# A two-layer graph network with residual norms on one core: source indices kept on chip, GpSimd's gathers written out over all groups, four input buffers in place of two

## What is computed

```python
def _cgconv(x, src, dst, attr, Wf, bf, Ws, bs):
    z = jnp.concatenate([x[dst], x[src], attr], axis=-1)
    m = jax.nn.sigmoid(z @ Wf + bf) * jax.nn.softplus(z @ Ws + bs)
    return jax.ops.segment_sum(m, dst, num_segments=N) + x

h = leaky_relu(graph_norm(_cgconv(x, ...)))        # layer 1
h = leaky_relu(graph_norm(_cgconv(h, ...)))        # layer 2
x = layernorm(x + h)
Wh = x @ W + b                                     # layer 3
Wr, Wc = Wh[src], Wh[dst]
sim = sum(Wr * Wc) / max(|Wr| * |Wc|, eps)
base = adj_v * softplus(deg_coeff[0] * deg_v + deg_coeff[1]) * (src != dst)
pos = segment_sum(base * relu(sim) * Wc, src); neg = segment_sum(-base * relu(-sim) * Wc, src)
out = layernorm(x + scale * (c[0] * pos + c[1] * neg + c[2] * Wh))
```

## Time and profile before

| | us |
|---|---|
| median of 3 runs | 11558.24 |
| lowest, highest run | 11554.88, 11572.58 |
| span of the profiled execution, first to last instruction | 11550.1 |
| GpSimd (POOL) busy | 7691.0 (67%) |
| TensorE (PE) busy | 4750.4 (41%) |
| VectorE (DVE) busy | 4365.6 (38%) |
| ScalarE (ACT) busy | 2260.1 (20%) |

### The profile page before, as it was taken

The page is one execution under the profiler, slowest core; times in us unless marked ns, Lnnn a source line. Parts: engine busy times, 40 slices in busy tenths (PEclk is TensorE's granted clock), DMA queues, the critical chain, the costliest instruction groups (busy, mean ns, idle before and its releaser), DMA issues. The chain is left out here.

```text
span 11550.1 us, 89590 instructions
## 1 busy us (share of the span) xinstructions
PE 4750.4 (41%) x15982; PEld 2985.0 (26%) x15982; DVE 4365.6 (38%) x7054; ACT 2260.1 (20%) x3460; POOL 7691.0 (67%) x6875
## 2 busy tenths in 40 slices
PE   0067776777206666777641222222222222222221
PEld 0033333333103333333321222222222222222221
DVE  2333333333303333333333344444444444444445
ACT  0033333333103333333321101001001010010100
POOL 5556656555435665666653688888888888888885
PEclk9977778878557777777775555555555555555555
DMA  7233333333203333333320233333333333333333
GB/s 278 66 93 97 96 97 96 96 96 94 89 25 87 93 93 89 93 94 91 93 72 20 32 36 37 36 36 37 36 37 36 36 37 36 37 36 36 37 36 75
DMA packets 869598, 790.23 MB, mean 68 GB/s; under 512 B 483674, under 2 KB 621802, under 8 KB 868298
## 3 DMA queue, kind: packets, MB, share of 16 engines
q0 software_dynamic: 398432, 244.82, 17.4%
q1 hardware_dynamic: 461928, 480.85, 13.7%
q10 hardware_dynamic: 9218, 64.36, 1.4%
HBM read 547.94 MB, written 241.38 MB: 68 GB/s over the span
## 5 line engine op out<-in xcount | busy, mean ns | idle before, releaser
L659 POOL DMA_INDIRECT by_src<-arena,put_idx x1568 | 2483.8, 1584 | 482.0 <-issue 482.0
L583 POOL DMA_INDIRECT G<-h_rows,idx x1568 | 1542.1, 983 | 978.2 <-issue 480.6
L583 POOL DMA_INDIRECT G<-in_x,idx x1470 | 1452.8, 988 | 971.0 <-issue 469.5
L760 PE MATMUL ps_gv<-ident,arena 128*128 128x128 f32 x1568 | 385.4, 427 | 3729.8 <-issue 3709.7
L583 POOL DMA_INDIRECT G<-wh_rows,idx x1568 | 1530.0, 976 | 484.3 <-issue 443.1
L760 PEld LDWEIGHTS ps_gv<-ident,arena 128*128 128x128 f32 x1568 | 307.5, 224 | 3790.6 <-issue 3769.7
L1036 DVE TENSOR_TENSOR_SCAN xd_t<-same,xd_t,ps_inj 128x512 f32<-128x512 bf16 x588 | 751.6, 1278 | 1377.5 <-remote 951.5
L712 PE MATMUL ps_gv<-attr,w_attr 65*128 65x512 f32 x1568 | 1089.0, 832 | 391.0 <-DMA attr<-in_attr_t 361.7
L715 PE MATMUL ps_gv<-arena,w_src 128*128 128x512 f32 x1568 | 1034.6, 797 | 0.0
L1179 DVE TENSOR_SCALAR put_idx<-arena,drop 128x8 int32<-128x8 f32 x196 | 45.5, 232 | 2269.4 <-DMA by_src<-arena,put_idx 2269.4
L1059 DVE TENSOR_SCALAR arena<-ps_gv 128x512 f32<-128x512 f32 x392 | 267.5, 682 | 1624.8 <-remote 1071.3
(11 more groups left out here) (161 smaller groups left out, 7026.5 us busy)
## 6 DMA issues: line engine op xcount, KB each, us to landing
inj<-first_edge_rows SPq DMA_DIRECT2D x588, 256.0 KB
running_sums<-arena SPq DMA_DIRECT2D x392, 256.0 KB
same<-same_dst SPq DMA_DIRECT2D x1176, 64.0 KB
first_edge_rows<-zeros ACTq DMA_DIRECT2D x56, 896.0 KB
attr<-in_attr_t SPq DMA_DIRECT2D x392, 128.0 KB
same_sum<-same_dst SPq DMA_DIRECT2D x784, 64.0 KB
G<-h_rows,idx POOLq DMA_INDIRECT x1568
G<-wh_rows,idx POOLq DMA_INDIRECT x1568
```

Of the source, the lines that this page charges most:

```text
L583: pool.indirect_dma_start(out_, None, table_in, bass.IndirectOffsetOnAxis(ap=index, axis=0)).then_inc(s, 16)
L659: pool.indirect_dma_start(acc_d[a], bass.IndirectOffsetOnAxis(ap=put_idx[:, buf, k:k + 1], axis=0), put[:, buf, k * D:(k + 1) * D], None, ...
L760: mm = pe.transpose(spread[:, buf, k], src_f[:, buf, k:k + 1].to_broadcast([P, P]), ident[:])
```

## The change

- `src_idx`, 128 x 1568 int32, takes all source indices in the first load of the kernel. The 588 loads of `idx` go, and the 14 of `src_ahead`. GpSimd's gathers take columns of `src_idx` that are fixed numbers, so its program is written out: 196 groups without a loop in each of the three passes, and the 14 steps of the gather ahead.
- `inj`, `same`, `attr` and `G` have NB = 4 buffers. The other tiles keep two. Loops over groups run 49 trips of 4.
- `same_sum` and its 784 loads go: both scans read `same`. So the second half of `load_rows` waits for the *sums* of group k-2 (`s_sumt`) where it waited for the scan before (layer 3 still waits for the scan).
- SyncE's order in layers 1 and 2: attributes of k+1, rows and flags of k+2, the ahead row of k, the store of the sums of k-3.
- `same_all` moves into the shared arena, which is cut to 16800 columns.

```diff
+            load(src_idx[:], src_g, s_srcs)
             load(last_i, block_last.to_broadcast([P, SEARCH]), s_search)
...
-            load(src_i, src_e, s_edges)
...
                 def load_rows(h, buf):
-                    g = h * 2 + buf
-                    sp.wait_ge(s_scan, done(layer, h, buf, 2))
+                    g = h * NB + buf
+                    sp.wait_ge(s_injt, done(layer, h, buf, NB))
                     load(inj[:, buf], inj_groups[ds(g, 1)].rearrange("a p c -> p (a c)"), s_load[buf])
-                    load_same(same, s_load, g, buf)
+                    sp.wait_ge(s_scan if layer == 2 else s_sumt, done(layer, h, buf, NB))
+                    for half in range(2):
+                        load(same[half * D:(half + 1) * D, buf],
+                             same_groups[ds(g + half * GROUPS, 1), :].to_broadcast([D, COLS]), s_load[buf])
                 def load_ahead(h, buf):
-                    if buf and layer < AHEAD:
-                        sp.wait_ge(s_gt, done(layer, h, buf, 2))
+                    if buf % 2 and layer < AHEAD:
+                        sp.wait_ge(s_gt, done(layer, h, buf, NB))
...
-                pipeline(sp, (load_idx, -1), (load_rows, -1), (load_ahead, 0), (load_attr, 1), (load_again, 2),
-                         (store_sums, 4))
+                load_attr(0, 0)
+                pipeline(sp, (load_attr, -1), (load_rows, -2), (load_ahead, 0), (store_sums, 3))
...
-                with pool.Fori(0, PAIRS) as i:
-                    for buf in range(2):
-                        gather_group(i, buf)
+                for g in range(GROUPS):
+                    gather_group(g)
...
-                        wait(s_idx[buf], h * 16 + 16 * (layer * PAIRS + 1))
-                        if layer < 2:
-                            wait(s_gt, done(layer, h, buf, 2))
-                        else:
-                            wait(s_used, done(0, h, buf, 2))
+                        wait(s_gt if layer < 2 else s_used, done(layer if layer < 2 else 0, h, buf, NB))
...
-                    dve.wait_ge(s_same_sum[buf], loaded_one(32, layer, h))
-                    v.tensor_tensor_scan(sum_t[:, buf], same_sum[:, buf], msg, sum_t[:, 1 - buf, COLS - 1:COLS],
+                    v.tensor_tensor_scan(sum_t[:, buf % 2], same[:, buf], msg, sum_t[:, 1 - buf % 2, COLS - 1:COLS],
```

More of the change, by code:

```diff
@@ L103, in two, with each @@
             return [sem(f"{name}_{i}") for i in range(2)]
+        def each(name):
+            return [sem(f"{name}_{i}") for i in range(NB)]
         def dram(name, shape, dt=F32):
@@ L158, in gnn @@
         seam_row = sb("seam_row", [P, D])
-        idx = sb("idx", [P, 2, SLOTS], I32)
-        inj = sb("inj", [P, 2, SLOTS * D])
-        same = sb("same", [P, 2, COLS], BF16)
-        same_sum = sb("same_sum", [P, 2, COLS], BF16)
-        attr = sb("attr", [2 * DA + 1, 2, COLS])
-        G = sb("G", [P, 2, SLOTS * D])
+        inj = sb("inj", [P, NB, SLOTS * D])
+        same = sb("same", [P, NB, COLS], BF16)
+        attr = sb("attr", [2 * DA + 1, NB, COLS])
+        G = sb("G", [P, NB, SLOTS * D])
         xd_t = sb("xd_t", [P, 2, COLS])
-        arena = sb("arena", [P, 17600])
+        arena = sb("arena", [P, 16800])
         def carve():
@@ L418, in pipeline @@
                     steps.begin(i - head, per)
-                step(i, 0)
-                step(i, 1)
+                for buf in range(n):
+                    step(i, buf)
             if steps:
@@ L423, in pipeline @@
                 steps.begin()
-            for k in range(2 * tail, 2 * pairs + max(lags)):
-                step(k // 2, k % 2)
+            for k in range(n * tail, n * trips + max(lags)):
+                step(k // n, k % n)
             if steps:
@@ L511, in load_same @@
[L511 to L518 removed]
+                    if buf % 2 and layer < AHEAD:
+                        sp.wait_ge(s_gt, done(layer, h, buf, NB))
+                        load(G[:, buf, (SLOTS - 1) * D:],
+                             ahead_pairs[:, ds(h * (NB // 2) + buf // 2, 1)].rearrange("p a f -> p (a f)"),
+                             s_ahead_in[buf // 2])
@@ L520, in store_sums @@
+                def load_attr(h, buf):
+                    sp.wait_ge(s_gates, done(layer, h, buf, NB))
+                    load(attr[0:2 * DA, buf], attr_t[ds(h * NB + buf, 1)].rearrange("a k c -> k (a c)"), s_attr[buf])
                 def store_sums(h, buf):
-                    g = h * 2 + buf
+                    g = h * NB + buf
                     sp.wait_ge(s_sums, done(layer, h, buf))
-                    load(sums_groups[ds(g, 1)].rearrange("a p c -> p (a c)"), sums[:, buf], s_stored[buf])
@@ L585, in gather_ahead @@
             def gather_ahead(begin, end):
-                with pool.Fori(begin, end) as i:
+                for i in range(begin, end):
                     for buf in range(2):
-                        wait(s_aidx[buf], i * 16 + 16)
                         wait(s_ahead_st[buf], i * 16 + 16)
                         for c in range(CH):
-                            gather(agg[:, buf, c * D:(c + 1) * D], x, get_nodes[:, buf, c:c + 1], s_ahead[buf])
+                            pair = (i * 2 + buf) * CH + c
+                            gather(agg[:, buf, c * D:(c + 1) * D], x, src_of(2 * pair + 1, SLOTS - 1), s_ahead[buf])
+            pool.wait_ge(s_srcs, 16)
             pool.wait_ge(s_end_idx, 1)
@@ L624, in _ @@
                     stages.append((lambda h, buf, c=c: put_column(layer, h, buf, c), 0 if layer else 3))
-                pipeline(pool, *stages, pairs=CP)
+                pipeline(pool, *stages, n=2, trips=CP)
                 table_in = (x, h_d, wh_d)[layer]
@@ L655, in add_run @@
                         half = a // (ACCS // 2)
-                        if a % (ACCS // 2) == 0 and (run or buf or not at_start(h)):
+                        if a % (ACCS // 2) == 0 and (run or g):
                             wait(s_added[half], added(h, buf, run))
@@ L1203, in _ @@
             steps.end()
-            with dve.Fori(1, PAIRS) as i:
-                steps.begin(i - 1, 26)
+            with dve.Fori(1, TRIPS) as i:
+                steps.begin(i - 1, 13 * NB)
                 last_layer(i)
-            steps.end(PAIRS - 1, 26)
+            steps.end(TRIPS - 1, 13 * NB)
             with dve.Fori(0, CP) as i:
```

226 lines of the change are left out of this document (107 added, 119 removed).

## The result

The changed kernel took 11652.5 us (median of three runs, 11635.7 to 11656.5) against 11558.2 before: 1.0081 of it, 95% interval 1.0058 to 1.0103. It is slower by 0.8%, where I had forecast 1.9% faster (11345). The profiled execution has a span of 11654.7 us, 104.6 more than before.

The account below looks back on a forecast made before the run. It took GpSimd to pace the group passes, TensorE not far behind. Setup -25, first waits -18, straight-line code 0, layer 2 -442, layer 1 +271 sum to -214 against 11550: 11336, taken as 11345 us; range 11060 to 11700.

Parts of the forecast that it names:

- Setup: Start of the kernel: indices become the first load, so GpSimd's gathers ahead start earlier; 25 us off.
- Straight-line code: GpSimd's program without loops in the three passes: neither gain nor loss, taken as 0.
- Layer 1: Layer 1's pass: TensorE waits for the ahead row in odd groups; 27.5 us a pair, 271 us more.
- Layer 2: Layer 2's pass: the index wait goes; 10.6 us a group, 2078 us against 2520, 442 off.
- Layer 3 and the stages: Layer 3's pass stays at 25.4 us a group apart from its first wait; norm stages are left alone.
- Rival 1: Layers 1 and 2: ahead row's chain with late releases outweighs layer 2's gain; 30 us a pair, 11785 us, chance 0.20.
- Rival 3: Layers 1 and 2: late releases, not index loads, make the group times, which remain; 11515 us, chance 0.07.
- Rival 2: Layers 1 and 2 both at GpSimd's pace, the ahead row landing in time; about 10510 us, chance 0.04.
- rival 4: All three passes: each loop trip costs a branch of 1.06 us; 312 us more off, 11030 us, chance 0.03.
- The signs: Profile marks for the forecast, and three against it: no L705 wait, layer 2 above 12 us a group, microsecond steps.
- the first waits: First group of each layer's pass: GpSimd's wait for its first indices goes; together 18 us off.

Follow-up runs that it names:

- e4: Kernel before with only the source indices kept on chip and GpSimd's groups written out without a loop: 11290.2 us, 0.9662 of before.
- e11: The change with the ahead row first in SyncE's order, on chip 9: 11150.2 us, 0.9654 of before.
- e1: The change with the ahead row first in SyncE's order, on chip 1: 11235.4 us, 0.961 of before.
- e3: The change with the ahead row first, and layer 2's two products with w_dst left out: layer 2 took 2341 us.
- e7: The change with the ahead row first and the sums turned a group later, on chip 6: 10620.3 us, 1.0037 of before.
- e17: The change with the ahead row first, GpSimd waiting for src_rows_turned only every second group in layers 1 and 2, chip 11: 10616.4 us, 1.0026 of before.
- e2: The change with the ahead row first, and half of the gathers in layer 2: layer 2 took 1320 us.
- e18: The change with the ahead row first, GpSimd in layers 1 and 2 waiting for earlier gathers to land, chip 11: 11168.9 us, 1.0555 of before.
- e15: The change with the ahead row first, layer 2 making only its products with w_attr, on chip 10: layer 2 took 2290 us.
- e16: The change with the ahead row first, 6 of 8 gathers a group in layer 2, on chip 10: layer 2 took 1784 us.
- e12: The change with the ahead row first and the sums turned a group later, on chip 9: 11136.8 us, 0.9645 of before.

## Why the prediction was wrong

- *Setup*, -25: right (-24.3). *Straight-line code*, 0: right for layer 3 (`e4`), and GpSimd's own steps in layer 2 are 2022 us in both kernels.
- *Layer 1*, +271: right in size (+273.5), in place (L693 of odd groups) and in its parts (9.7 us idle, 27.2 us a pair). `e11` shows the mechanism by taking it away on one chip: 486 us of layer 1 come back (and 459 in `e1` against the first result, on chips that may differ).
- *Layer 2*, -442: this is the step that failed. The sentence "GpSimd's own 10.3 us, if TensorE keeps below it" was true: the own steps came out at 10.3, and TensorE kept below it. Wrong was "I take 10.6 us a group": of the 489 us that GpSimd waited for `idx` or "remote", I let 442 go with the index loads and gave late releases 0.3 us a group. They cost 1.5, 294.8 us of GpSimd's stops in the pass. I had taken the name of a wait for its cause. A stop with the name `idx` was for the greater part a late release, with the index load's own time behind it: with the loads gone there are about as many stops (88 for 94), of 3.4 us in place of 5.3, and `e4`, which takes away the index loads and the loop alone, has 101 of 3.6. So 417.5 us of wait taken away brought 197. I had asked whether gathers without a pause would bring more late releases, and whether fewer DMAs would bring fewer. Neither shows: the "remote" idle times of ScalarE and VectorE are about what they were. That they were there already, at full size, is what I missed.
- *Layer 3 and the stages*, 0: +19 and +33, small but one way. The stages' part is mostly TensorE's larger rest of work after the last gather, 27 us more after layer 1. Layer 3's part is open: it was 4935 with two buffers on chip 1 (`e4`) and 4964 and 4948 with four (`e1`, `e3`), but 4945 against 4942 on chip 9.
- *Rival 1* came nearest. Its direction is right, and its 11.6 us a group for layer 2 is what was measured (11.8). Its price for layer 1, 30 us a pair, is not, nor is its place for the late releases, the ahead row's chain. It put the turn at 29.7 us a pair with layer 2 as forecast; with layer 2 at 11.8 us the forecast's own 27.5 was enough.
- *Rival 3* (late releases, not index loads, make the group times) is right in its cause and wrong in its number. On chips 6 and 11, without late releases, the kernel before is as fast with its index loads as `e7` and `e17` are without. So where releases are late, nearly all of the 2.5 us by which a group of layer 2 lies above GpSimd's own 10.3 hangs on them (by these totals, without a trace), and taking the loads away brings 1.0 of it. *Rival 2* and *rival 4* did not come.
- *The signs.* In layer 1 TensorE's wait at the turning of G came, with a granted clock of 0.75, and in the setup the first gather ahead at 19.7 us. None of the three that would have shown the forecast wrong did: layer 2 came to 11.8 us a group, and I had set the mark at 12, against a forecast of 10.6. A mark so wide misses the failure of the largest term.

From the forecast's -214 to the measured +105: 245 for layer 2, 33 for the stages, 19 for layer 3, 18 for the first waits, which were not found as a saving of their own, and 3 for layer 1 and the setup.

On chips without late releases I would estimate another size. Layer 1 of the change, at the 26.9 us a pair of the prediction's sum without them, is 2636 us against the 1998 of `e17`, so the change would stand near 10616 + 638 = 11250 us against 10588, 6% slower. This wasn't run. The two versions with the ahead row first that do the whole work and ran there are slower than before too, `e17` by 0.3% and `e7` by 0.4%.

**Still open.** What makes the releases late isn't known: the five chips differ, and nothing in the program does. Each chip was met in one set of runs, so a state of the machine at that time can't be told from a property of the chip.

Also open is whether it is the missing pause or the rate of gathers that counts, since `e2` has both more pauses and a lower rate, and `e17` and `e18` met a chip that has no stops. The numbers speak for a rate, though no run was made to test it. The stops of `e15` end once about 1.45 to 1.48 us have passed for each gather since the last stop (23.7 us for 16, 35.3 for 24, 46.5 for 32), and those of `e16` mostly lie 17.9 to 18.5 us apart, 1.49 to 1.54 for each of 12. GpSimd's own step is 1.29 us. What goes slower than 1.5 us an indirect DMA on average has hardly any stops: layer 1 of the change (27.4 us for 15, 1.83), `e2` (6.73 for 4, 1.68) and layer 3 (25.3 for 16, 1.58). So my estimate is that on such a chip something behind GpSimd gets through one indirect DMA in about 1.5 us, and that a stop is the time in which it catches up.

The best version is the change with the ahead row first and the sums a group later, 0.9645 of before on chip 9, though only 13 us below the ahead row first alone. It isn't better everywhere: the same kernel is 1.0037 of it on chip 6.

## What to carry over

When a load is put behind another on an in-order queue, it inherits the other's wait: look up who issues behind each new wait and who needs that, since two words in an order here undid 4% of gain. The name that the profile gives to a wait is that of the release that came last, and another can stand close behind it. So before a wait is counted as a gain, look at how often the engine stops, how far apart, and what the same stop costs where it carries another name: here the 22 "remote" stops beside the 70 for `idx` were the hint. And compare two kernels on one chip, with a pass that neither touches as the witness of what kind of chip it is: layer 1 was that here for the runs that change layer 2 alone.

## What the hardware showed that I had not expected

- Five chips are of two kinds for this kernel: 11548 to 11687 us and 10586 to 10588 us for the same program. Layer 3 takes 4932 to 4964 us on both; layers 1 and 2 of one kernel (`e7` and `e12`) take 2205 and 2306 us on the one and 1997 and 2020 on the other, 10% and 14% more.
- On the first kind, GpSimd's gathers in an unbroken row go with semaphore releases that are late for all engines, by the number of gathers and not by their bytes. Where 593 gathers and 135 pauses of 1.9 us share a millisecond (`e2`) this is all but gone; with no other pause GpSimd stands still for 13% to 14% of the time, at 650 to 680 gathers a millisecond. In the stop of `e15` that ends at 3686.37, after 4.62 us, VectorE starts again at 3685.54 after 10.67 us of "remote" idle time and ScalarE at 3685.60 after 2.30: the engines come free together.
- Gathers cost 0.95 us and the same step to the next, 0.30, on every chip.
